# One gathered column of every seventh block fetched row by row on SyncE, from byte offsets

## The reference

```python
edge_index = jnp.stack([src, dst])
h = jnp.maximum(_layernorm(x, axis=-1), 0.0)
x = x + _L0_gnn_ref(h, edge_index, edge_attr_64, ...)   # msg_in = concat(h_nodes[dst], h_nodes[src], h_edges)
h = jnp.maximum(_layernorm(x, axis=-1), 0.0)
x = x + _L1_gnn_ref(h, edge_index, ...)                 # e = a_src[src] + a_dst[dst]; msg = h[src] * alpha
```

## Time and profile before

| what | us |
|---|---|
| median of 3 runs (lowest to highest) | 4092.73 (4090.88 to 4094.87) |
| profiled execution, its own time | 4091.22 |
| its span from first to last instruction | 4089.1 |
| mean granted clock of PE, share of full speed | 0.838 |

### The profile page before, as it was taken

One profiled execution on the slowest core, in us unless ns is written; L12 is line 12 of the kernel. 1 busy time (PEld: TensorE's weight loads), 2 busy tenths in 40 slices (PEclk: granted clock), 3 DMA queues, 4 the chain that ended last, 5 costly groups with the idle time before them and its releaser, 6 DMA issues. The chain is left out here.

```text
span 4089.1 us, 126775 instructions
## 1 busy us (share of the span) xinstructions
PE 3382.9 (83%) x30848; PEld 2976.2 (73%) x30849; DVE 2517.0 (62%) x10511; ACT 2850.5 (70%) x5940; POOL 2965.8 (73%) x3134
## 2 busy tenths in 40 slices
PE   7789888999988899999947777777777778777777
PEld 4677777777777788888847777777777767766776
DVE  5752222222222256777748777777777777888888
ACT  6466565656556577788738777777777777877777
POOL 2677777777777777777737777777777777777774
PEclk8789999999899899999967777777777777777777
DMA  5322222222222233333342222222222222332332
GB/s 159 88 60 53 54 55 53 56 53 53 55 54 53 60 83 91 91 96 95 81 120 58 57 58 58 57 58 58 58 57 58 58 58 63 79 78 76 78 78 58
DMA packets 319769, 282.90 MB, mean 69 GB/s; under 512 B 143418, under 2 KB 242924, under 8 KB 319532
## 3 DMA queue, kind: packets, MB, share of 16 engines
q0 software_dynamic: 99456, 159.33, 15.9%
q1 hardware_dynamic: 139224, 79.62, 7.4%
q10 hardware_dynamic: 80852, 41.75, 3.5%
HBM read 249.58 MB, written 29.40 MB: 68 GB/s over the span
## 5 line engine op out<-in xcount | busy, mean ns | idle before, releaser
L541 POOL DMA_INDIRECT a_G<-Htab,idx x1554 | 1470.8, 946 | 526.3 <-issue 464.0
L541 POOL DMA_INDIRECT p_rows<-Btab,idx x1554 | 1471.4, 947 | 475.1 <-issue 473.4
L1799 PE MATMUL a_psA<-a_GP,a_S 128*128 128x132 f32 x4704 | 892.5, 365 | 2.7 <-DVE a_GP L1634 2.7
L1799 PEld LDWEIGHTS a_psA<-a_GP,a_S 128*128 128x128 f32 x4704 | 821.5, 268 | 8.2 <-DVE a_GP L1634 3.1
L1056 DVE TENSOR_TENSOR p_z<-p_psZ,p_rows 128x512 f32<-128x512 f32 x294 | 195.9, 689 | 829.4 <-SPq L746 679.6
L1206 ACT COPY p_ST<-p_psT 128x1024 bf16<-128x1024 bf16 x294 | 300.5, 1022 | 563.7 <-PE p_psT L1318 543.4
L1730 ACT CAST a_S<-a_Sb 128x512 f32<-128x512 bf16 x588 | 608.6, 1144 | 0.0
L1365 PE MATMUL p_psA<-p_msg,p_S 128*128 128x65 f32 x4704 | 589.9, 284 | 10.9 <-ACT p_S L1227 9.8
L1365 PEld LDWEIGHTS p_psA<-p_msg,p_S 128*128 128x128 f32 x4704 | 571.6, 201 | 16.5 <-issue 12.8
L1227 ACT CAST p_S<-p_Sb 128x1024 f32 (+1 forms) x294 | 582.6, 1982 | 0.0
L1341 PEld LDWEIGHTS p_psZ<-wc,p_s 128*128 128x128 f32 x2352 | 325.1, 206 | 204.7 <-issue 103.5
(11 more groups left out here) (212 smaller groups left out, 5165.8 us busy)
## 6 DMA issues: line engine op xcount, KB each, us to landing
arena<-in_ea SPq DMA_DIRECT2D x196, 256.0 KB
p_single<-Btab SPq DMA_DIRECT2D x1792, 0.2 KB
a_single<-Htab SPq DMA_DIRECT2D x1792, 0.5 KB
p_rows<-Btab,idx POOLq DMA_INDIRECT x1554
a_G<-Htab,idx POOLq DMA_INDIRECT x1554
Htab<-u_H ACTq DMA_DIRECT2D x49, 136.0 KB
arena<-Htab SPq DMA_DIRECT2D x7, 952.0 KB
n_x<-in_x SPq DMA_DIRECT2D x14, 448.0 KB, 4.0
```

The source lines that it names most:

```text
L541: pool.indirect_dma_start(out=rows[:, u * C + c, :], out_offset=None, in_=table, in_offset=bass.IndirectOffsetOnAxis(ap=idx[u][:, c:c + 1] ...
L1799: m = pe.matmul(psA[v][:, 0:HR], S32[v][:, c, :], GP[v][:, c, :], start=c == 0, stop=c == C - 1)
```

## The change

SP fetches its column in the last block of every round but the first, not only of every second one. It does so a round ahead: in round i it issues the 128 row DMAs of round i + 1, in 7 batches of 18 or 19, one behind each block, into one of two halves of the spare tile. `landed` waits for all rows of a round at the next round's first block, `place` copies them in the round's sixth block, and `placed` waits for the copy before the seventh. The numbers in `at` are no longer node numbers but byte offsets into the table: the opening multiplies them by the row size of either table on DVE and stores them in `offsets`, and the table is seen as bytes. The indices of 7 blocks come in one DMA of 28 KB a round, into one of two index tiles. Two smaller edits go with it: `flagt` shares the place of `x1`, and DVE waits for the flag rows' stores before `x1` is written first.

```diff
-BATCH = (12, 12, 12, 8, 12, 8, 12, 8, 12, 8, 12, 12)
+BATCH = (19, 18, 18, 18, 18, 18, 19)
+ROUNDS = NB // SLOTS
...
             run_pairs(sp, body, NG, 3)
+            sp.wait_ge(s_off, 18)
+            for n in range(2):
+                sp.dma_start(offsets[n], bytes_[n][:, :]).then_inc(s_off, 16)
+            sp.wait_ge(s_off, 50)
...
+            act.dma_start(nodes[:, :], t["single"]).then_inc(s_off, 16)
...
+                dve.wait_ge(s_off, 16)
+                for n, size in enumerate((4 * H, 4 * HROW)):
+                    dve.tensor_scalar(bytes_[n][:, :], nodes[:, :], size, None, ALU.mult).then_inc(s_off, 1)
...
-    def block(i, odd, u, used):
-        if due(16 * (i + 1 + turns)):
-            pool.wait_ge(s_idx[u], 16 * (i + 1 + turns))
+    def block(r, odd, u, used, whole=False):
+        if u == 0:
+            pool.wait_ge(s_idx[odd], 16 * (r + 1 + turns // 2))
...
-        for c in range(C - 1 if odd and u == SLOTS - 1 else C):
+        for c in range(C if whole or u < SLOTS - 1 else C - 1):
...
-        which = self.nc.values_load_multi_w_load_instructions(
-            self.at[0:1, first:first + BATCH[n]], engines=[sp.engine], min_val=0, max_val=NP - 1,
-            skip_runtime_bounds_check_because="indices of nodes")[1]
+        at = self.nc.values_load_multi_w_load_instructions(
+            self.k["at"][0:1, odd * P + first:odd * P + first + BATCH[n]], engines=[sp.engine], min_val=0,
+            max_val=(NP - 1) * self.size, skip_runtime_bounds_check_because="offsets of nodes")[1]
         for p in range(BATCH[n]):
-            sp.dma_start(self.spare[first + p:first + p + 1, :], self.table[bass.ds(which[p], 1), :]
-                         ).then_inc(self.s_row[n % 3], 16)
+            sp.dma_start(self.spare[first + p:first + p + 1, odd, :].bitcast(U8),
+                         self.table[bass.ds(at[p], self.size)].unsqueeze(0)).then_inc(self.s_row[n % 4], 16)
...
+    def landed(self, i):
+        for n in range(4):
+            self.sp.wait_ge(self.s_row[n], 16 * sum(BATCH[n::4]) * (i + self.before))
+            self.sp.sem_inc(self.s_turn, 1)
+
+    def step(self, i, odd, u, first, final):
+        if not first and u == 0:
+            self.landed(i)
+        if not first and u == SLOTS - 2:
+            self.place(i, odd)
+        if not final:
+            self.batch(i + 1, 1 - odd, u)
+            if u == 0 and not (isinstance(i, int) and i + 2 >= ROUNDS):
+                self.load(i + 2, odd)
...
+def load_idx(sp, t, k, i, odd):
+
+    sp.dma_start(k["idx"][odd][:, :], t["src"].rearrange("(i p) c -> i p c", p=P)[bass.ds(i, 1)]
+                 .rearrange("o p c -> (o p) c")).then_inc(k["slots"][0][odd], 16)
```

More of the change, by code:

```diff
@@ L549, in gather_blocks @@
     for u in range(SLOTS):
-        block(0, False, u, None)
+        block(0, 0, u, None, whole=True)
     if s_table is not None:
@@ L554, in gather_blocks @@
     for u in range(SLOTS):
-        block(1, True, u, used[u])
-    with pool.Fori(1, NB // SPAN) as r:
+        block(0, 1, u, used[u])
+    with pool.Fori(1, ROUNDS // 2) as r:
         used = used_by(r * SPAN, SPAN)
@@ L559, in gather_blocks, with __init__ @@
             for u in range(SLOTS):
[L560 removed]
+                block(r, odd, u, used[odd * SLOTS + u])
 class Rows:
[L566 to L568 removed]
+    def __init__(self, nc, sp, k, table, offsets, spare, to, s_used, s_turn, turn):
+        self.nc, self.sp, self.k, self.offsets, self.spare, self.to = nc, sp, k, offsets, spare, to
+        self.size = 4 * table.shape[1]
+        self.table = table.rearrange("n f -> (n f)").bitcast(U8)
+        self.s_used, self.s_turn = s_used, s_turn
@@ L569, in __init__, with load, batch @@
         self.s_at, self.s_row, self.s_to = k["singles"]
[L570 to L575, removed]
+        self.before = (ROUNDS - 1) * turn
+    def load(self, i, odd):
+        self.sp.dma_start(self.k["at"][0:1, odd * P:(odd + 1) * P], self.offsets[bass.ds(i, 1), :]).then_inc(self.s_at, 16)
+    def batch(self, i, odd, n):
         sp, first = self.sp, sum(BATCH[:n])
@@ L601, in placed @@
+    def placed(self, i):
+        self.sp.wait_ge(self.s_to, 16 * (i + self.before))
         self.sp.sem_inc(self.s_turn, 1)
-def gathers(r, odd, u, turns):
-    if u < SLOTS - 1:
[L607 to L618, removed]
@@ new lines, in step, with gathers @@
+    def step(self, i, odd, u, first, final):
[7 more added lines that the diff above has]
+                self.load(i + 2, odd)
+def gathers(i, u, turns):
+    if u < SLOTS - 1:
+        return 16 * C * (i + 1 + turns)
+    return (16 * (C + (C - 1) * (turns - 1)) if turns else 0) + 16 * (C - 1) * i + 16 * C
@@ L633, in arrived, with feed_blocks @@
+def load_idx(sp, t, k, i, odd):
+    sp.dma_start(k["idx"][odd][:, :], t["src"].rearrange("(i p) c -> i p c", p=P)[bass.ds(i, 1)]
+                 .rearrange("o p c -> (o p) c")).then_inc(k["slots"][0][odd], 16)
+def feed_blocks(nc, sp, t, s_used, s_turn, s_ready, k, side, turns, then, singles):
+    _, s_g, s_side = k["slots"]
+    def arrived(i, u):
+        sp.wait_ge(s_g[u], gathers(i, u, turns))
         sp.sem_inc(s_turn, 1)
@@ L639, in feed_blocks @@
         side(u, u)
-    singles.load(0)
+    singles.load(1, 1)
     then()
@@ L645, in blocks @@
         for u in range(SLOTS):
[L646 to L650, removed]
+            if u == SLOTS - 1 and not first:
+                singles.placed(i)
+            arrived(i, u)
+            if u == 0 and not final:
+                load_idx(sp, t, k, i + 1, 1 - odd)
             if not (final if u >= SLOTS - 2 else first):
@@ L655, in blocks @@
                 side(i * SLOTS + u + 2, (u + 2) % SLOTS)
-            step_singles(singles, r, odd * SLOTS + u, final)
+            singles.step(i, odd, u, first, final)
     def used_at(i):
@@ L742, in blocks @@
                 sp.sem_inc(s_eardy, 1)
-            if odd and u == SLOTS - 1:
-                singles.placed(r)
-            sp.wait_ge(s_g[u], gathers(r, odd, u, 0))
+            if u == SLOTS - 1 and not first:
+                singles.placed(i)
+            sp.wait_ge(s_g[u], gathers(i, u, 0))
             sp.sem_inc(s_ready, 1)
-            load_idx(u if final else (i + 1) * SLOTS + u, u)
-            step_singles(singles, r, odd * SLOTS + u, final)
+            if u == 0:
+                load_idx(sp, t, k, 0 if final else i + 1, 1 - odd)
+            singles.step(i, odd, u, first, final)
     def used_at(i):
@@ L834, in _ @@
         def _(sp):
-            singles = Rows(nc, sp, t, k, Btab, single, k["at"], rows[:, SLOTS * C - 1, :], s_z, s_turn, 0)
-            feed_messages(nc, sp, t, idx, ea, s_s1, s_turn, s_ready, s_eardy, s_table, k, singles)
+            singles = Rows(nc, sp, k, Btab, offsets[0], single, rows[:, SLOTS * C - 1, :], s_z, s_turn, 0)
+            feed_messages(nc, sp, t, ea, s_s1, s_turn, s_ready, s_eardy, s_table, k, singles)
         @block.gpsimd
@@ L1092, in body @@
                     update_mean(row - MEAN)
+                if isinstance(row, int) and row == NORM:
+                    dve.wait_ge(s_fst, 32)
                 if up(row - NORM):
@@ L1428, in sums @@
                                  Htab.rearrange("(g w p) f -> g p w f", w=2 * GW, p=P)[g]).then_inc(s["al"], 16)
-            singles = Rows(nc, sp, t, k, Htab, single, k["at"], G[:, SLOTS * C - 1, :], s["GP"], s["turn"], 1)
-            feed_blocks(nc, sp, t, idx, s["GP"], s["turn"], s["ready"], k, side, NB // SLOTS, sums, singles)
+            singles = Rows(nc, sp, k, Htab, offsets[1], single, G[:, SLOTS * C - 1, :], s["GP"], s["turn"], 1)
+            feed_blocks(nc, sp, t, s["GP"], s["turn"], s["ready"], k, side, NB // SLOTS, sums, singles)
         @block.gpsimd
```

75 lines of the change are left out of this document (32 added, 43 removed).

## The result

| what | us |
|---|---|
| changed kernel, median of 4 runs (lowest to highest) | 4601.23 (4595.31 to 4602.56) |
| kernel before, median of 4 runs beside it | 4091.81 (4089.92 to 4094.87) |
| ratio, 95% interval | 1.1241 (1.1222 to 1.1261) |
| profiled execution after, its span, granted clock | 4595.31, 4593.5, 0.798 |

A forecast was written before the change was run, and what follows sets the result against it. GpSimd's issue of gathers was taken to bound the kernel, with SyncE becoming the bound after the change. 4091 + 327 (message pass) + 305 (attention pass) - 5 - 11 + 1 = 4708, say 4710 us; range 4580 to 4880.

The forecast's parts named there:

- The bound moved to SyncE: Both passes: SyncE needs 81.4 and 80.6 us per round, GpSimd 68.7, so SyncE becomes the bound; slower 93%.
- row transfers, 256: SyncE's fetched rows per double round: 0.341 us each without the arithmetic, 87.3 us after 54.6 before.
- register loads, 14: SyncE's loads of row offsets per double round, mostly starting off multiples of four words: 51.1 us against 10.4 before.
- rounds' ends: SyncE placing the fetched column, its semaphores, loading row numbers and waits for landed rows: 5.6 us per double round, before 2.3.
- index DMAs: SyncE's index transfers per double round: 14 small ones become 2, 7.8 us become 1.1.
- the rest: SyncE's edge or flag loads, ready signals, due times and loop's end per double round: stays at 17.7 us.
- the lower of the two ends: Eighteen-value load off a multiple of four: 3.85 us by SyncE's rows, 4.06 by GpSimd's; 3.93 taken.
- The ends of both passes: First rounds have nothing to place or wait for, -5 us; the last 7 blocks no longer wait for gathers, -11.
- The load that catches up with the next multiple of four: SyncE's loads then all cost about 1.75 us, GpSimd stays the bound, 4059 us or a little above; chance 5%.
- The move goes too: SyncE's row transfers lose the move with the arithmetic: 18 us less per double round, about 4220 us; chance 4%.
- the arithmetic stays: SyncE's row transfers still need address arithmetic: 20 us more per double round, about 5255 us; chance 3%.
- TensorE's clock: Paced more slowly, TensorE may be granted less clock; at 0.72 late in the message pass +70 us, 4780; chance 6%.

## Why the prediction was right, and where its sizes were off

**The bound moved to SyncE.** Right, step by step: gathers no longer follow at 1.25 us but wait for VectorE's release, SyncE's waits for gathers shrink to almost nothing, and the chain is L600 and L596. From the trace after, first ready signal to first ready signal, the 27 rounds of a pass with batches average 78.84 us (message) and 78.88 (attention). The forecast was 81.4 and 80.6, so it was 3 and 2% too dear.

**The sum per double round,** 590.5 to 748.8 us of the trace after, added up from SyncE's instructions there:

| term, us | forecast | measured | what was off |
|---|---|---|---|
| row transfers, 256 | 87.3 | 85.0 | 0.332 a row on average, not 0.341 |
| register loads, 14 | 51.1 | 50.0 | 18 values 3.84, not 3.93 |
| rounds' ends | 5.6 | 4.6 | |
| index DMAs | 1.1 | 0.7 | |
| the rest | 17.7 | 17.4 | |
| waits | 0 | 0.3 | |
| sum | 162.8 | 158.0 | |

The largest error is the row. The step that was off takes 0.042 us for the gap behind each of three instructions and drops one gap with the arithmetic. With move and DMA at 0.257 us, the steady 0.324 leaves 0.067 for two gaps, 0.033 each: the arithmetic had taken more than its share of the gap. The mean of 0.332 holds batches of 18 rows of up to 6.2 us among those of 5.74. For the loads of the message pass the lower of the two ends, SyncE's own (0.45 + 17 x 0.20 = 3.85), was nearly exact. In the attention pass the same loads of 18 took 3.94 us in the median and the 14 loads 51.8 us a double round on average, so there the forecast's 3.93 and 51.1 hold. The 3.93 is not quite the middle that the prediction calls it: between 3.85 and 4.06 that is 3.955. No stall came from the four waits for landed rows: SyncE's waits are 0.3 us in the double round. One reading of the prediction does not hold: indices issued a whole round ahead still came late for GpSimd, by up to 5.8 us in 12 waits of the message pass, since GpSimd runs nearly a round ahead of SyncE's ready signals. With SyncE the bound this cost nothing more, and with SyncE relieved such a wait occurred once, for 1.4 us.

**The time.** 27 rounds add 254.7 us in the message pass, where 327 were forecast, and 268.1 in the attention pass, where 305 were. The ends of both passes give back 16.4 us (10.8 + 5.6); forecast, 5 + 11. The opening, taken at +1, is 2 us shorter (the first block is ready at 123.4 us, before at 125.4). 254.7 + 268.1 - 16.4 - 2 = 504.4 us. (The kernel before's own 27 rounds, taken the same way, average 69.41 and 68.95 us, so 69.3 was a fair base for both.) The 2.56 and 1.72 us too many per round, 27 times each, are 116 us, about what lies between 4710 and the profiled 4595; the base, the opening and rounding make up the rest and nearly cancel. In the message pass every term of work was taken somewhat too high. The forecast's own terms reached down to 4610, and 4601 lies in the range only because its lower end had been widened to 4580. The bound, the path and the two main terms, these to 3%, were foreseen; that the range held was partly luck.

**The rivals.** The load that catches up with the next multiple of four is excluded: 18 values take 3.84 us off one and 1.45 to 1.58 on one. Its arithmetic was useful all the same: it put the kernel with such loads at 4059 us, and the one that has them measures 4066. "The move goes too" is excluded by the rows of L600, "the arithmetic stays" as well. TensorE's clock did fall, but its busy share did not rise. Four stretches of the trace after, in the columns of the earlier trace rows, early and late in either pass:

```profile
300.00:1300.00 1000.00, 837.67 (x7728) 720.02 (x7727) 232.71 (x528) 533.42 (x533) 689.03 (x731) 0.87 0.19 49
1400.00:2100.00 700.00, 598.18 (x5769) 509.30 (x5770) 339.88 (x1280) 444.53 (x656) 451.56 (x477) 0.92 0.27 71
2500.00:3500.00 1000.00, 689.13 (x5677) 637.97 (x5674) 676.96 (x3166) 657.72 (x1845) 663.92 (x704) 0.70 0.20 52
3600.00:4450.00 850.00, 586.73 (x4847) 541.37 (x4845) 621.76 (x2884) 565.06 (x1571) 557.07 (x588) 0.71 0.24 63
```

The granted clock is 0.87 and 0.92 in the message pass, 0.06 and 0.05 below, while TensorE is 0.84 and 0.85 busy. Late in the pass it stays at 0.92, far from the 0.72 that this rival needed. In the attention pass it is 0.70 and 0.71 where the earlier trace rows has 0.72 and 0.76, while TensorE is 0.69 busy; SyncE, not TensorE, makes the chain there.

**The rule on register loads.** The rows decide between the Trainium skill's price of about 200 ns per register even in bulk ("Runtime: NRT & Kernel Launch", section "Instruction fetch mechanics") and the price by fours: loads off a multiple of four show 3.84 / 18 = 0.21 us, as the page says, and loads of 20 on one 1.36 / 20 = 0.068 us, which it does not. All these loads read `at`, a tile in SBUF; none here reads registers from HBM.

## What to carry to other kernels

Work that goes to an idle-looking queue is to be summed instruction by instruction, register loads included, against that queue's free time in one period of the loop; here 46 us were free and 65 were added. Start a register load of many values on a multiple of four words, and let every batch be whole fours: here that alone was worth 535 us. A queue that signals readiness in the same stream as its extra work passes its overdraft on to every engine behind it, so the engine that was relieved wins nothing.

## What the runs showed of the hardware that was not expected

A register load off a multiple of four costs 0.20 us per value and does not catch up within 19 values; on one, 16 to 20 values take 1.0 to 1.8 us in the median. The step between the two is 2.3 to 2.5 us for the same 18 values. A load that starts on a multiple of four but is not whole fours costs more than the next longer one that is: in one round 18 values took 1.58 us from word 20 and 20 values 1.21 us from word 0.

On three chips the kernel before takes 6840 to 6950 us instead of 4093, 1.67 times as long, at a granted clock of 0.69 to 0.70. The same instruction there has the same median and a far longer tail. A row's move and DMA in the kernel with all batches on multiples of four, on such a chip:

```profile
L600 SPq MOVE p_single<-Btab x3456: 2/29/1408, 122.0 to 3267.5; - x192
L600 SPq DMA_DIRECT2D p_single<-Btab x3456: 2/228/1396, 122.0 to 3268.9; - x192
```

After, the longest move is 38 ns. On the slow chip one of these moves in ten takes about 0.7 us and the longest 1.4 us, and the mean of a move is 0.10 us. VectorE's and GpSimd's busy time is what it is elsewhere (2531.8 and 2942.0 us in this kernel, 2514.4 and 2942.0 on the ordinary chip), but no engine is full (TensorE, the busiest, is 57% busy). What stalls the sequencers there, these runs do not tell.
